# Differential attention, per-token attention and routed low-rank layers in one kernel: steps moved by one or two chunks in the per-token phase, one POOL step and a prefetch depth moved in the causal phase

## The chip, the cores and the metric

One core of a Trainium2 chip runs the whole program. The metric is the device time of one execution in microseconds (us), from several executions of the same program. The chip's engines are named as the profile names them: PE (TensorE, matmuls, with PEld for its weight loads), DVE (VectorE), ACT (ScalarE), POOL (GpSimd) and SP (which only issues DMAs here). Each engine works through its own list of instructions in order, and semaphores tie the lists together.

## The reference, cut to what matters

The input has 2 batches of 1024 tokens with 128 numbers each. Four layers follow one another, each added to its input after a layernorm:

```python
x = x + attn_a(layernorm(x))   # 16 heads, each with two causal softmax maps over 1024 tokens,
                               # out = softmax1 @ v - lambda * softmax2 @ v, rms norm, projection
x = x + ffn(layernorm(x))      # base matmul plus one of four low-rank experts per token
x = x + attn_b(layernorm(x))   # per token, below
x = x + ffn(layernorm(x))

# attn_b: H = 16 heads, C = 64 channels; everything is inside one token
Q = (x @ Wq + bq).reshape(b, s, H, C) * inv_sqrt_c
K = (x @ Wk + bk).reshape(b, s, H, C)
V = (x @ Wv + bv).reshape(b, s, H, C)
scores = einsum('bshq,bshk->bshqk', Q, K)       # a 64 x 64 outer product per token and head
scores = where(triu(ones((C, C)), 1), -inf, scores)
w = softmax(scores, axis=-1)
attn = einsum('bshqk,bshk->bshq', w, V)
return attn.reshape(b, s, HID) @ Wo + bo
```

In `attn_b` the score of query channel i and key channel j is the product q[i]*k[j], so the largest score of a row is the larger of q[i]*max(k[0..i]) and q[i]*min(k[0..i]). The kernel gets these maxima from a running maximum and a running minimum of the keys.

## The kernel before, in words

The program runs phases one after the other: a1 (load, layernorm, q/k/v), a2 (causal attention), a3 (rms norm and projection), f1, b (per-token attention), f2. The change touches a2 and b.

**Phase b** works on 16 tiles of 128 tokens. The scores of a tile are cut into 24 chunks, `c` = 0 to 23, of 256 to 2048 numbers per partition (token); chunks 0 to 15 are half 0 of the queries, 16 to 23 are half 1. The sizes in order are 2048, 256, 2048, 512, 2048, 768, 2048, 1024, 2048, 1280, 2048, 1536, 2048, 1792, 2048, 2048, and then 2048, 256, 1792, 512, 1536, 768, 1280, 1024. Every chunk passes through all four engines:

- DVE multiplies queries by keys into `p_ring` (L969, "product"), four chunks ahead (`AHEAD = 4`) of its own second step;
- POOL subtracts the row maxima `m` in place (L1059, "shift");
- ACT takes the exponential in place (L1097);
- PE adds up the exponentials by identity matmuls into a PSUM bank (L1160, the denominators), DVE multiplies them by the values into `ev_ring` (L1017), and PE adds those up in another bank (L1160, the numerators).

Written out by hand around the chunks are the steps that happen once or twice in a tile. Numbers such as `FINISH1_AT` name the chunk after which an engine does them; `it` is the tile in work:

- keys of tile it+1 on PE (`KEY_AT`), copied out of PSUM by ACT (`KEY_TAKEN_AT`); the same keys head by head on PE (`HJ_AT`, "hj"), scanned by DVE into running maxima and minima (`SCAN_AT`, L976 and L978), reordered by ACT with two copies (`TURN_BACK_AT`, L1083, "turned back"), and multiplied by the queries on DVE (`maxima`, L990, L991, L993; half 0 of the next tile after chunk 20, half 1 of this tile after chunk 12);
- the queries of half 1 on PE after chunk 11 (`Q1_AT`), those of half 0 of the next tile after chunk 19;
- the reciprocals of the denominators on ACT as exp(-ln(x)), with a table load ahead of either function (`invert`, L1075 and L1077): half 0 after chunk 20 of the tile, half 1 after chunk 4 of the next one;
- `finish` on DVE (L999), which multiplies the summed numerators by these reciprocals: half 0 after chunk 19, half 1 after chunk 3 of the next tile; then the output projection on PE (`PROJECT_AT`, L1169) and the residual addition on DVE (`RESIDUAL_AT`, L1004).

A linear step on PE is a matmul (L1125, which the profile shows as two records) and a small one for the bias (L1126). The first `maxima` product goes to `m`, the second to a PSUM bank `t`; before, `t` is bank `T_BANK`, which keys, hj and the projection use as well, and which is why `maxima` of half 1 waited for the keys to be taken, and hj for `maxima`.

**Phase a2** works on 16 jobs (a batch and a group of four score maps). In a job PE goes through 12 blocks of keys (`at` = 0 to 11, four score matmuls each, L492, 48 steps), ACT takes exponentials (L547), POOL zeroes the future part of the eight blocks on the diagonal (`mask`, L384, at 0, 1, 2, 3, 8, 9, 10, 11) and PE multiplies by the values (L505). Between the score matmuls PE works off a list of 26 items: 24 "max" items (scores for the row maxima, L449 and L453, each reduced by DVE, L564, from 256 to 1024 numbers wide), one "rows" item (L462, which puts the maxima of the next job into rows, after POOL has split them into three bf16 parts: `split`, L374 and L377) and one "turn" item. Two pairs of PSUM banks take the items in turn, so that an item on PE needs the one two places ahead of it to be reduced on DVE. `EARLY` is how many max items of job n+2 are worked off in job n; `EARLY_ROWS` is behind how many of these the rows item stands. After items 8 to 11 of a job DVE also does a `pad` (L573).

Of the kernel before, what the change touches and what calls it, by code (L numbers as in the profile page):

```python
# [44 lines left out]
H = 16  # L45
# [12 lines left out]
class Count:  # L58
# [8 lines left out]
    def at(self, it, k):  # L67

        return it * self.per + (self.first + k)
# [232 lines left out]
def phase_a2(nc, rows_q, rows_k, rq, rk_of_group, rk, v1, att, k, queries_spread, keys_spread):  # L302
# [4 lines left out]
    JOBS = BATCH * GROUPS  # L307
    with ExitStack() as ctx:
# [9 lines left out]
        ps = ctx.enter_context(nc.psum_tensor("a2_ps", [P, 8, 512], F32))  # L318
# [2 lines left out]
        U, G = len(units), len(groups)  # L321
        STEPS = 4 * G
        ST_SLOTS, ST_BANK, O_BANK, ITEM_BANK = 3, 0, 3, 4
        EARLY, EARLY_ROWS, TURN_ITEM, PAD_ITEM = 5, 3, 6, 8
        DIAGONAL = [at for at, (half, sbk) in enumerate(groups) if sbk * P >= 512 * half]
        masked = sem("masked", len(DIAGONAL))
        ready = sem("ready")
# [37 lines left out]
        @block.gpsimd  # L365
        def _(pool):
            def split(n):

                pool.wait_ge(item_taken.sem, number[("max", n, U - 1)] + 1)
                if n >= 1:  # L370
                    pool.wait_ge(item_psum.sem, number[("rows", n - 1, 0)] + 1)
                for part in range(3):
                    rows = mrows[:, :, M_ROW + 4 * part:M_ROW + 4 * part + 4]
                    nc.gpsimd.tensor_copy(rows, negm[:, n % 2]).then_inc(split_step.sem, 1)  # L374
                    pool.wait_ge(split_step.sem, split_step.at(n, 2 * part + 1))
                    if part < 2:
                        nc.gpsimd.tensor_tensor(negm[:, n % 2], negm[:, n % 2], rows, ALU.subtract).then_inc(split_step.sem, 1)  # L377
                        pool.wait_ge(split_step.sem, split_step.at(n, 2 * part + 2))

            def mask(n, at):  # L380

                pool.wait_ge(exp_done.sem, exp_done.at(n, 4 * at + 4))
                block_diagonal = ex[:, (G * n + at) % 3, :, 0:P]
                nc.gpsimd.affine_select(block_diagonal, block_diagonal, [[0, 4], [1, P]], ALU.is_ge, 0.0, base=0,  # L384
                                        channel_multiplier=-1).then_inc(masked.sem, 1)

            def combine(n):

                g, b = n // BATCH, n % BATCH
                pool.wait_ge(divided.sem, divided.at(n, 2))  # L390
                nc.gpsimd.tensor_scalar(oh[:, :, 1, :], oh[:, :, 1, :], k["lam"][:], None, ALU.mult).then_inc(out_step.sem, 1)
                pool.wait_ge(out_step.sem, out_step.at(n, 1))
                dst = att[:, b * NT:(b + 1) * NT, g * 2 * A_V:(g + 1) * 2 * A_V].rearrange("p n (v c) -> p n v c", v=2)
                heads = oh[:].rearrange("p (n v) s c -> p n v s c", n=NT)
                nc.gpsimd.tensor_tensor(dst, heads[:, :, :, 0, :], heads[:, :, :, 1, :], ALU.subtract).then_inc(out_step.sem, 1)

            nc.gpsimd.memset(mrows[:], 0.0).then_inc(ready.sem, 1)
            nc.gpsimd.tensor_scalar(k["wqkv"][:, 0, :], k["wqkv"][:, 0, :], 0.125, None, ALU.mult).then_inc(scaled.sem, 1)
            nc.gpsimd.tensor_scalar(k["bias"][0:HID // 32, :], k["bias"][0:HID // 32, :], 0.125, None, ALU.mult).then_inc(scaled.sem, 1)
            pool.wait_ge(scaled.sem, 2)  # L400
            for part in range(3):
                nc.gpsimd.tensor_copy(bias_parts[:, part, :], k["bias"][:]).then_inc(bias_step.sem, 1)
                pool.wait_ge(bias_step.sem, bias_step.next(0))
                if part < 2:
                    nc.gpsimd.tensor_tensor(k["bias"][:], k["bias"][:], bias_parts[:, part, :],
                                            ALU.subtract).then_inc(bias_step.sem, 1)
                    pool.wait_ge(bias_step.sem, bias_step.next(0))
            pool.wait_ge(ready.sem, 1)
            split(0)
            for n in range(JOBS):  # L410
                for at in DIAGONAL:
                    mask(n, at)
                    if at == 2 and n >= 1:
                        combine(n - 1)
                    if at == 9 and n + 1 < JOBS:
                        split(n + 1)
            combine(JOBS - 1)
            pool.wait_ge(out_step.sem, out_step.at(JOBS - 1, 2))

# [438 lines left out]
def phase_b(nc, x_all, k):  # L858
# [11 lines left out]
    BEGIN = (0, 16)  # L870
# [3 lines left out]
    Q_BANK, T_BANK, V_BANK, ACC_BANK = 0, 1, 2, 4  # L874
    HALF = HID // 2
    INVERT0_AT, INVERT1_AT = 20, 4
    FINISH0_AT, FINISH1_AT, PROJECT_AT, RESIDUAL_AT = 19, 3, 4, 6
    XT_AT, KEY_AT, KEY_TAKEN_AT = 5, (7, 9), (10, 12)
    HJ_AT, SCAN_AT, TURN_BACK_AT = (13, 15), (14, 16), 18
    Q1_AT, Q0_AT, V1_AT, V0_AT = 11, 19, 16, 23  # L880
    with ExitStack() as ctx:
        sb = lambda n, s, d=F32: ctx.enter_context(nc.sbuf_tensor("b_" + n, s, d))
# [19 lines left out]
        ps = ctx.enter_context(nc.psum_tensor("b_ps", [P, 8, 512], F32))  # L902
# [8 lines left out]
        key_taken = sem("key_taken", 2)  # L911
# [3 lines left out]
        m_step = sem("m_step", 6)  # L915
# [22 lines left out]
        def chunk(ring, c):  # L938

            half, j0, n = CH[c]  # L940
            return ring[:, c % ring.shape[1], 0:ROWS * n * H].rearrange("p (j i h) -> p j i h", j=ROWS, h=H)
# [9 lines left out]
        def over_queries(t, c):  # L951

            return t.unsqueeze(2).broadcast_to([P, ROWS, CH[c][2], H])
# [7 lines left out]
        def _(dve):  # L961
# [16 lines left out]
                nc.vector.tensor_tensor_scan(kmin[:, cols], k["reset_min"][:, 0:HALF], ps[:, T_BANK], 0.0,  # L978
                                             ALU.max, ALU.min).then_inc(scan_done.sem, 1)

            def maxima(it, half, last=False):

                q = ps[:, Q_BANK].rearrange("p (i h) -> p i h", h=H)
                t = ps[:, T_BANK].rearrange("p (i h) -> p i h", h=H)
                at = lambda r: r[:, half * FIRST:(half + 1) * FIRST, :]
                dve.wait_ge(q_psum.sem, q_psum.at(it, half + 1))
                dve.wait_ge(turned_back.sem, turned_back.at(it, 2))
                if half == 1 and not last:
                    dve.wait_ge(key_taken.sem, key_taken.at(it + 1, 2))
                nc.vector.tensor_tensor(m[:, half], q, at(kmaxr), ALU.mult).then_inc(m_step.sem, 1)  # L990
                nc.vector.tensor_tensor(t, q, at(kminr), ALU.mult).then_inc(m_step.sem, 1)  # L991
                dve.wait_ge(m_step.sem, m_step.at(it, 3 * half + 2))
                nc.vector.tensor_tensor(m[:, half], t, m[:, half], ALU.max).then_inc(m_step.sem, 1)  # L993
# [12 lines left out]
            def tile(it, buf, first, last):  # L1006
                for c in range(N):
                    coming = (it, buf, c + AHEAD) if c + AHEAD < N else None if last else (it + 1, 1 - buf, c + AHEAD - N)
                    begins = coming and coming[2] in BEGIN
                    if coming and not begins:  # L1010
                        multiply(*coming, first and c + AHEAD < N)
                    if c == 0:
                        dve.wait_ge(v_psum.sem, v_psum.at(it, 2))
                    dve.wait_ge(exp_done.sem, exp_done.at(it, c + 1))
                    if c >= EV_SLOTS or not first:
                        dve.wait_ge(ev_summed.sem, ev_summed.at(it, c - EV_SLOTS + 1))
                    nc.vector.tensor_tensor(chunk(ev_ring, c), chunk(p_ring, c), over_queries(values(c), c),  # L1017
                                            ALU.mult).then_inc(ev_done.sem, 1)
                    if begins:
                        maxima(coming[0], BEGIN.index(coming[2]), last)  # L1020
                        multiply(*coming, first and c + AHEAD < N)
                    if not first and c == FINISH1_AT:
                        finish(it - 1, 1)
                    if not first and c == RESIDUAL_AT:
                        residual(it - 1)
                    if c == FINISH0_AT:
                        finish(it, 0)
                    if not last and c in SCAN_AT:
                        scans(it + 1, SCAN_AT.index(c))
# [91 lines left out]
        def _(pe):  # L1121
# [51 lines left out]
            def tile(it, buf, first, last):  # L1173
                for c in range(N):
                    half = CH[c][0]
# [11 lines left out]
                        queries(it, buf, 1)  # L1187
                    if not last and c in HJ_AT:
                        if c == HJ_AT[0]:
                            pe.wait_ge(m_step.sem, m_step.at(it, 6))  # L1190
                        keys_by_head(it + 1, 1 - buf, HJ_AT.index(c))
                    if not last and c == V1_AT:
                        pe.wait_ge(ev_done.sem, ev_done.at(it, 16))
# [9 lines left out]
            for s in range(TILES // FT):  # L1203
                pe.wait_ge(xn_ready.sem, s + 1)
                for n in range(FT):
                    last = nc.tensor.transpose(ps[:, ACC_BANK + s, n * P:(n + 1) * P], xn[:, s * FT + n, :], k["ident"][:])
# [8 lines left out]
            vals(0, 0, 1)  # L1215
            vals(0, 0, 0)
            all_tiles(pe, tile)
            project(TILES - 1)

# [107 lines left out]
```

## Time and profile before

| | |
|---|---|
| device time, median of 3 | 2248.83 us (2248.59 to 2249.04) |
| the profiled execution: its own time | 2247.19 us |
| its span, first to last instruction | 2245.5 us |
| mean granted TensorE clock, share of full speed | 0.937 |
| busy in the span | PE 1893.1, DVE 1888.0, POOL 1415.5, ACT 1106.6 us |
| first and last POOL shift of phase b | 711.8 and 2172.3 us |
| first and last mask of phase a2 | 90.6 and 587.8 us |

Read a busy time of a whole program as a mean over phases: a2 and b are bounded by different engines. Where the profile says what ended an idle time, the engine named is the one whose result came last.

### The profile page before, as it was taken

To read this page: it belongs to the slowest core of one execution; us is meant where nothing else is said; L and a number is where in the kernel's file an instruction comes from. 1 tells how busy PE (TensorE), PEld (TensorE's weight loads), DVE (VectorE), ACT (ScalarE), POOL (GpSimd) and SP (SyncE) were. 2 spreads that over 40 slices of the span, in tenths; PEclk is the share of its full clock that TensorE was granted. 3 is DMA by queue.
4 is the path that set the end of the run, shared out by engine and by line. 5 is a ranking of instruction groups with operands and counts; after the bars stand their busy time and mean duration, and the time that the engine had idled before them with its cause. 6 is when DMAs were issued, how large, how long until landed. Compare 5 with 4: busy or idle time off the path is not lost. (4 is left out here: it accounts for less than half of the span.)

```text
span 2245.5 us, 35597 instructions
## 1 busy us (share of the span) xinstructions
PE 1893.1 (84%) x14176; PEld 1405.2 (63%) x14226; DVE 1888.0 (84%) x1607; ACT 1106.6 (49%) x1448; POOL 1415.5 (63%) x661
## 2 busy tenths in 40 slices
PE   2899999999565978889889898888888989889886
PEld 1344444443253767767778787776777777777785
DVE  6877888777345989989899899998999989999884
ACT  2366666666412454454545544445544555444540
POOL 5122222222113987978879788797897987979871
PEclk8899999999866999999999999999999989999996
DMA  3300000000000000000000000000000000000000
GB/s 96 61 7 6 8 8 8 5 5 1 1 0 0 1 1 1 1 2 1 1 2 1 1 1 2 1 1 2 1 1 2 1 1 1 2 1 1 1 1 19
DMA packets 10981, 14.46 MB, mean 6 GB/s; under 512 B 4656, under 2 KB 7632, under 8 KB 10672
## 3 DMA queue, kind: packets, MB, share of 16 engines
q1 hardware_dynamic: 9264, 11.31, 2.1%
q8 instruction: 126, 2.06, 0.4%
q10 hardware_dynamic: 1536, 0.63, 0.1%
q14 instruction: 55, 0.45, 0.1%
HBM read 4.57 MB, written 1.05 MB: 3 GB/s over the span
## 5 line engine op out<-in xcount | busy, mean ns | idle before, releaser
L1059 POOL TENSOR_TENSOR b_p_ring<-b_p_ring,b_m 128x2048 f32<-128x2048 f32 (+7 forms) x384 | 1251.4, 3300 | 244.3 <-DVE b_p_ring L969 243.0
L1097 ACT ACTIVATE b_p_ring<-b_p_ring 128x2048 f32<-128x2048 f32 (+7 forms) x384 | 532.3, 1411 | 654.1 <-POOL b_p_ring L1059 652.5
L1160 PE MATMUL b_ps<-k_ident,b_ev_ring 128*128 128x128 f32 (+6 forms) x4608 | 606.5, 283 | 162.9 <-DVE b_ev_ring L1017 157.5
L1160 PEld LDWEIGHTS b_ps<-k_ident,b_ev_ring 128*128 128x128 f32 (+6 forms) x4608 | 510.0, 139 | 237.2 <-DVE b_ev_ring L1017 211.2
L1017 DVE TENSOR_TENSOR b_ev_ring<-b_p_ring,b_ps 128x2048 f32<-128x2048 f32 (+7 forms) x384 | 634.1, 1655 | 5.7 <-PE b_ps L1126 4.0
L969 DVE TENSOR_TENSOR b_p_ring<-b_ps,b_key 128x2048 f32<-128x2048 f32 (+7 forms) x384 | 634.4, 1660 | 0.0
L1160 PE MATMUL b_ps<-k_ident,b_p_ring 128*128 128x128 f32 (+6 forms) x4608 | 588.0, 279 | 18.3 <-ACT b_p_ring L1097 12.6
L1160 PEld LDWEIGHTS b_ps<-k_ident,b_p_ring 128*128 128x128 f32 (+6 forms) x4608 | 521.9, 138 | 28.5 <-ACT b_p_ring L1097 12.9
L547 ACT ACTIVATE a_ex<-a_ps 128x512 f32<-128x512 f32 (+3 forms) x768 | 333.0, 497 | 200.5 <-PE a_ps L492 191.0
L564 DVE TENSOR_REDUCE a_negm<-a_ps 128x1 f32<-128x768 f32 (+7 forms) x384 | 353.3, 953 | 75.6 <-PE a_ps L453 72.7
L384 POOL TENSOR_SCALAR_AFFINE_SELECT a_ex<-a_ex 128x512 f32<-128x512 f32 x128 | 81.6, 638 | 372.6 <-ACT a_ex L547 371.1
L449 PE MATMUL a_ps<-rk,rq 128*128 128x512 bf16 (+3 forms) x751 | 190.8, 335 | 31.3 <-DVE rk L573 16.6
L492 PE MATMUL a_ps<-rq,rk 128*128 128x512 bf16 (+3 forms) x735 | 202.9, 329 | 6.9 <-ACT a_ex L547 5.5
L505 PE MATMUL a_ps<-a_ex,v 128*32 128x512 f32 (+3 forms) x1536 | 163.9, 499 | 1.1 <-POOL a_ex L384 1.1
L492 PEld LDWEIGHTS a_ps<-rq,rk 128*128 128x128 bf16 x768 | 64.0, 98 | 149.0 <-ACT a_ex L547 116.6
L1125 PE MATMUL b_ps<-k_wqkv,b_xt 128*128 128x512 f32 x256 | 138.1, 622 | 5.2 <-DVE b_kmin L978 2.4
L449 PEld LDWEIGHTS a_ps<-rk,rq 128*128 128x128 bf16 x768 | 66.5, 99 | 82.5 <-DVE a_negm L564 33.4
L999 DVE TENSOR_TENSOR b_oT<-b_ps,b_rden 128x512 f32<-128x512 f32 x32 | 22.1, 692 | 107.9 <-ACT b_rden L1077 107.9
L453 PE MATMUL a_ps<-k_mask,k_ident_b 128*128 128x128 bf16 x512 | 93.5, 224 | 0.0
L1083 ACT COPY b_kmaxr<-b_kmax 128x1024 f32<-128x1024 f32 x16 | 32.1, 2007 | 102.0 <-DVE b_kmin L978 102.0
L453 PEld LDWEIGHTS a_ps<-k_mask,k_ident_b 128*128 128x128 bf16 x512 | 50.3, 101 | 45.8 <-issue 5.0
L1126 PEld LDWEIGHTS b_ps<-bias,ones 3*128 3x128 bf16 x128 | 11.6, 91 | 101.9 <-issue 101.9
(163 smaller groups left out, 1076.8 us busy)
## 6 DMA issues: line engine op xcount, KB each, us to landing
rk_of_group<-rows_k SPq DMA_DIRECT2D x96, 32.0 KB, 2.0
rq<-rows_q SPq DMA_DIRECT2D x42, 64.0 KB, 2.4
k_wqkv<-in_wqkv SPq DMA_DIRECT2D x1, 2048.0 KB, 8.5
out<-x_all SPq DMA_DIRECT2D x4, 256.0 KB, 2.4
k_wo<-in_wo SPq DMA_DIRECT2D x1, 512.0 KB, 9.3
rq<-rows_q SPq DMA_DIRECT2D x12, 32.0 KB, 1.9
k_w_attn<-in_w_attn ACTq DMA_DIRECT2D x1, 192.0 KB, 2.8
k_reset_max<-in_reset_max ACTq DMA_DIRECT2D x1, 128.0 KB, 4.8
```

The lines of the kernel that those rows point to most:

```text
L449: nc.tensor.matmul(dst[:, 512 * at + c:512 * at + c + w], rq[:, g, b, t * P:(t + 1) * P], rk[:, n % 3, hh, c:c + w], start=True, stop=c + ...
L453: last = nc.tensor.matmul(dst[:, c:c + P], k["ident_b"][:], k["mask"][:], start=False, stop=True)
L492: nc.tensor.matmul(dst[:, 0:hi - lo], rk[:, n % 3, hh, sbk * P:(sbk + 1) * P], rq[:, g, b, lo:hi], start=True, stop=True).then_inc(st_psum ...
L505: last = nc.tensor.matmul(ps[32 * hh:32 * hh + 32, O_BANK, lo - 512 * half:512], v1[:, b * NT + sbk, 2 * g + hh // 2, :], ex[:, (G * n + a ...
L547: nc.scalar.activation(ex[:, (G * n + at) % 3, hh, 0:hi - lo], ps[:, ST_BANK + s % ST_SLOTS, 0:hi - lo], ACT.Exp).then_inc(exp_done.sem, 1)
L564: nc.vector.tensor_reduce(negm[:, n % 2, t, heads[0]:heads[-1] + 1], src, X, ALU.max, negate=True).then_inc(item_taken.sem, 1)
L969: nc.vector.tensor_tensor(chunk(p_ring, c), over_rows(ps[:, Q_BANK], c), over_queries(key[:, buf, j0:j0 + ROWS, :], c), ALU.mult).then_inc ...
L1017: nc.vector.tensor_tensor(chunk(ev_ring, c), chunk(p_ring, c), over_queries(values(c), c), ALU.mult).then_inc(ev_done.sem, 1)
L1059: nc.gpsimd.tensor_tensor(pc, pc, over_rows(m[:, half].rearrange("p i h -> p (i h)"), c), ALU.subtract).then_inc(shifted.sem, 1)
L1097: nc.scalar.activation(pc, pc, ACT.Exp).then_inc(exp_done.sem, 1)
L1125: nc.tensor.matmul(ps[:, bank], xt[:, buf], k["wqkv"][:, i, cols], start=True, stop=False)
L1160: last = nc.tensor.matmul(ps[0:width, bank, b // IB * P:(b // IB + 1) * P], rows[:, r, b:hi].rearrange("p i h -> p (i h)"), k["ident"][:], ...
```

## The change

In phase a2, five max items early become seven, the rows item moves two places back among them (so that it keeps its place in the list), and POOL's `split` for the next job stands ahead of the mask at 9 instead of behind it. In phase b, `finish` of half 1 moves from chunk 3 to 5, the projection from 4 to 6, the residual from 6 to 8, the keys from (7, 9) to (9, 11), their copies from (10, 12) to (12, 14), hj from (13, 15) to (14, 16), the scans from (14, 16) to (15, 17), and the turned copies from 18 to 20, where they stand behind `invert` of half 0. The scratch of `maxima` moves from `T_BANK` to the bank that sums the denominators of the same half; `maxima` of half 1 no longer waits for the keys of the next tile to be taken, and hj waits for that copy instead of for `maxima`. No instruction is added or taken away.

```diff
-        EARLY, EARLY_ROWS, TURN_ITEM, PAD_ITEM = 5, 3, 6, 8
+        EARLY, EARLY_ROWS, TURN_ITEM, PAD_ITEM = 7, 5, 6, 8
...
                 for at in DIAGONAL:
+                    if at == 9 and n + 1 < JOBS:
+                        split(n + 1)
                     mask(n, at)
                     if at == 2 and n >= 1:
                         combine(n - 1)
-                    if at == 9 and n + 1 < JOBS:
-                        split(n + 1)
...
-    FINISH0_AT, FINISH1_AT, PROJECT_AT, RESIDUAL_AT = 19, 3, 4, 6
-    XT_AT, KEY_AT, KEY_TAKEN_AT = 5, (7, 9), (10, 12)
-    HJ_AT, SCAN_AT, TURN_BACK_AT = (13, 15), (14, 16), 18
+    FINISH0_AT, FINISH1_AT, PROJECT_AT, RESIDUAL_AT = 19, 5, 6, 8
+    XT_AT, KEY_AT, KEY_TAKEN_AT = 5, (9, 11), (12, 14)
+    HJ_AT, SCAN_AT, TURN_BACK_AT = (14, 16), (15, 17), 20
...
-            def maxima(it, half, last=False):
+            def maxima(it, half):
...
-                t = ps[:, T_BANK].rearrange("p (i h) -> p i h", h=H)
+                t = ps[:, ACC_BANK + 2 * half + 1].rearrange("p (i h) -> p i h", h=H)
...
-                if half == 1 and not last:
-                    dve.wait_ge(key_taken.sem, key_taken.at(it + 1, 2))
...
-                            pe.wait_ge(m_step.sem, m_step.at(it, 6))
+                            pe.wait_ge(key_taken.sem, key_taken.at(it + 1, 2))
```

What stands where on ACT, from chunk 18 to chunk 21 of a tile of phase b. Before:

```order
L1097 ACTIVATE b_p_ring<-b_p_ring 128x1792
L1083 COPY b_kmaxr<-b_kmax 128x1024
L1083 COPY b_kminr<-b_kmin 128x1024
L1097 ACTIVATE b_p_ring<-b_p_ring 128x512
L1097 ACTIVATE b_p_ring<-b_p_ring 128x1536
L1075 ACT_TABLE_LOAD
L1075 ACTIVATE b_rden<-b_ps 128x512
L1077 ACT_TABLE_LOAD
L1077 ACTIVATE b_rden<-b_rden 128x512
L1097 ACTIVATE b_p_ring<-b_p_ring 128x768
```

Of the changed kernel, whose lines stand two lower here (L1095 is L1097 of before, L1081 is L1083, L1073 and L1075 are L1075 and L1077):

```order
L1095 ACTIVATE b_p_ring<-b_p_ring 128x1792
L1095 ACTIVATE b_p_ring<-b_p_ring 128x512
L1095 ACTIVATE b_p_ring<-b_p_ring 128x1536
L1073 ACT_TABLE_LOAD
L1073 ACTIVATE b_rden<-b_ps 128x512
L1075 ACT_TABLE_LOAD
L1075 ACTIVATE b_rden<-b_rden 128x512
L1081 COPY b_kmaxr<-b_kmax 128x1024
L1081 COPY b_kminr<-b_kmin 128x1024
L1095 ACTIVATE b_p_ring<-b_p_ring 128x768
```

The two turned copies moved from ahead of the exponentials of chunks 19 and 20 and of the reciprocals to behind them.

DVE in a tile inside the loop, from its second step of chunk 3 on (the 512-wide L1017). Before:

```order
L1017 TENSOR_TENSOR b_ev_ring<-b_p_ring,b_ps 128x512
L997 ISA
L998 ISA
L999 TENSOR_TENSOR b_oT<-b_ps,b_rden 128x512
L969 TENSOR_TENSOR b_p_ring<-b_ps,b_key 128x2048
```

Of the changed kernel, where L1015 is L1017 of before and L997 is L999:

```order
L1015 TENSOR_TENSOR b_ev_ring<-b_p_ring,b_ps 128x512
L969 TENSOR_TENSOR b_p_ring<-b_ps,b_key 128x2048
L1012 REGISTER_ALU
L1015 TENSOR_TENSOR b_ev_ring<-b_p_ring,b_ps 128x2048
L969 TENSOR_TENSOR b_p_ring<-b_ps,b_key 128x1280
L1012 REGISTER_ALU
L1015 TENSOR_TENSOR b_ev_ring<-b_p_ring,b_ps 128x768
L995 ISA
L996 ISA
L997 TENSOR_TENSOR b_oT<-b_ps,b_rden 128x512
```

`finish` of half 1 moved behind the products of chunks 8 and 9 and the second steps of chunks 4 and 5.

POOL in phase a2, in a job in the middle (three masks, at 3, 8 and 9, then the split of the next job). Before:

```order
L395 TENSOR_TENSOR att<-a_oh 128x8x16
L384 AFFINE_SELECT a_ex<-a_ex 128x4x128 x3
L374 CAST a_mrows<-a_negm 128x8x4
L377 TENSOR_TENSOR a_negm<-a_negm,a_mrows 128x32
L374 CAST a_mrows<-a_negm 128x8x4
L377 TENSOR_TENSOR a_negm<-a_negm,a_mrows 128x32
L374 CAST a_mrows<-a_negm 128x8x4
L384 AFFINE_SELECT a_ex<-a_ex 128x4x128 x5
```

Of the changed kernel:

```order
L395 TENSOR_TENSOR att<-a_oh 128x8x16
L384 AFFINE_SELECT a_ex<-a_ex 128x4x128 x2
L374 CAST a_mrows<-a_negm 128x8x4
L377 TENSOR_TENSOR a_negm<-a_negm,a_mrows 128x32
L374 CAST a_mrows<-a_negm 128x8x4
L377 TENSOR_TENSOR a_negm<-a_negm,a_mrows 128x32
L374 CAST a_mrows<-a_negm 128x8x4
L384 AFFINE_SELECT a_ex<-a_ex 128x4x128 x6
```

The five small instructions of the split moved ahead of one mask.

## Rows read from the trace of the kernel before

**Rows 1.** Windows, chunk 0 to chunk 0: PE, PEld, DVE, ACT, POOL busy, clock, DMA

```profile
983.66:1076.50 92.84, 80.45 (x616) 68.51 (x616) 85.53 (x62) 45.59 (x37) 78.23 (x24) 0.97 0.01 2
...
1168.89:1261.70 92.81, 83.96 (x616) 71.97 (x616) 85.52 (x62) 45.57 (x37) 78.18 (x24) 0.93 0.01 2
```

**Rows 2.** Waits in phase b (720 to 2190 us): total us, times, longest

```profile
DVE b_oT L999 <- ACT b_rden L1077: 107.9, 32, 6.0
ACT b_kmaxr L1083 <- DVE b_kmin L978: 91.9, 15, 6.4
...
DVE b_ev_ring L1017 <- PE b_ps L1126: 4.0, 8, 1.4
```

**Rows 3.** Timeline of DVE: start us, us, instruction [idle before it <-releaser]

```profile
961.02 1.75 DVE L969 TENSOR_TENSOR b_p_ring<-b_ps,b_key 128x1536 f32<-128x1536 f32 x1
...
977.01 0.69 DVE L999 TENSOR_TENSOR b_oT<-b_ps,b_rden 128x512 f32<-128x512 f32 x1 [3.57 <-ACT b_rden L1077]
...
979.28 0.68 DVE L990 TENSOR_TENSOR b_m<-b_ps,b_kmaxr 128x512 f32<-128x512 f32 x1
...
1005.51 0.69 DVE L999 TENSOR_TENSOR b_oT<-b_ps,b_rden 128x512 f32<-128x512 f32 x1 [3.54 <-ACT b_rden L1077]
...
1038.34 0.68 DVE L990 TENSOR_TENSOR b_m<-b_ps,b_kmaxr 128x512 f32<-128x512 f32 x1
```

**Rows 4.** Timeline of DVE at the end of phase b

```profile
2184.86 0.69 DVE L999 TENSOR_TENSOR b_oT<-b_ps,b_rden 128x512 f32<-128x512 f32 x1 [6.04 <-ACT b_rden L1077]
```

**Rows 5.** Timeline of ACT, same columns

```profile
967.24 2.01 ACT L1083 COPY b_kmaxr<-b_kmax 128x1024 f32<-128x1024 f32 x1 [6.39 <-DVE b_kmin L978]
969.16 2.05 ACT L1083 COPY b_kminr<-b_kmin 128x1024 f32<-128x1024 f32 x1
...
973.14 1.28 ACT L1075 ACT_TABLE_LOAD   x1
...
976.34 0.63 ACT L1077 ACTIVATE b_rden<-b_rden 128x512 f32<-128x512 f32 x1
...
1023.92 1.49 ACT L1097 ACTIVATE b_p_ring<-b_p_ring 128x1536 f32<-128x1536 f32 x1 [1.06 <-POOL b_p_ring L1059]
...
1030.27 0.57 ACT L1090 COPY b_key<-b_ps 128x512 f32<-128x512 f32 x1
```

**Rows 6.** Timeline of POOL: stretches that begin at chunks 20, 8 and 16

```profile
962.85 3.46 POOL L1059 TENSOR_TENSOR b_p_ring<-b_p_ring,b_m 128x1536 f32<-128x1536 f32 x1 [2.48 <-DVE b_p_ring L969]
...
1008.48 33.01 POOL L1059 TENSOR_TENSOR b_p_ring<-b_p_ring,b_m 128x2048 f32<-128x2048 f32 x8 [0.64 <-DVE b_p_ring L969]
1042.72 10.51 POOL L1059 TENSOR_TENSOR b_p_ring<-b_p_ring,b_m 128x2048 f32<-128x2048 f32 x4 [1.23 <-DVE b_p_ring L969]
```

**Rows 7.** Timeline of POOL: single shifts, of chunk 6 and of chunk 12

```profile
1000.95 4.55 POOL L1059 TENSOR_TENSOR b_p_ring<-b_p_ring,b_m 128x2048 f32<-128x2048 f32 x1
...
1023.83 4.59 POOL L1059 TENSOR_TENSOR b_p_ring<-b_p_ring,b_m 128x2048 f32<-128x2048 f32 x1
```

**Rows 8.** Timeline of PE: the queries of half 1 after chunk 11

```profile
1035.53 1.02 PE L1125 MATMUL b_ps<-k_wqkv,b_xt 128*128 128x512 f32 x2
1036.49 0.38 PE L1126 MATMUL b_ps<-bias,ones 3*128 3x512 bf16 x1
```

**Rows 9.** Waits of the whole span: PE for POOL's split

```profile
PE a_ps L462 <- POOL a_mrows L374: 19.4, 15, 2.3
```

**Rows 10.** Timeline of PE: one rows item of phase a2

```profile
337.16 0.61 PE L462 MATMUL a_ps<-k_ident_b,a_mrows 128*128 128x128 bf16 x8 [1.22 <-POOL a_mrows L374]
```

**Rows 11.** Timeline of POOL: the mask at 9 and the split's last instruction

```profile
335.00 0.64 POOL L384 TENSOR_SCALAR_AFFINE_SELECT a_ex<-a_ex 128x512 f32<-128x512 f32 x1 [1.83 <-ACT a_ex L547]
...
336.81 0.21 POOL L374 CAST a_mrows<-a_negm 128x32 bf16<-128x32 f32 x1
```

**Rows 12.** Groups of reduces, 90 to 590 us: busy, mean ns | idle before

```profile
L564 DVE TENSOR_REDUCE a_negm<-a_ps 128x2 f32<-128x1024 f32 x30 | 35.4, 1216 | 1.3 <-PE a_ps L453 1.3
...
L564 DVE TENSOR_REDUCE a_negm<-a_ps 128x2 f32<-128x512 f32 x28 | 19.4, 692 | 20.2 <-PE a_ps L453 20.2
```

More of the change, by code:

```diff
@@ L1019, in tile @@
                     if begins:
-                        maxima(coming[0], BEGIN.index(coming[2]), last)
+                        maxima(coming[0], BEGIN.index(coming[2]))
                         multiply(*coming, first and c + AHEAD < N)
```

## The prediction

> **What bounds the kernel now.** I began with windows that each run from POOL's first shift of a tile to that of the next. A tile of phase b takes 92.8 us, and in it DVE is busy 85.5 us, POOL 78.2, PE 80.5 to 84.0 and ACT 45.6 [rows 1]. So DVE is nearest to being full, with about 7.3 us idle. Sixteen such tiles are some 1480 of the 2245.5 us. The list of waits in phase b says where DVE's idle time is: 107.9 us in 32 waits of L999 (`finish`) for the reciprocal on ACT, and 4.0 us in 8 waits for the values from PE [rows 2]. The reader is to see that almost nothing else holds DVE up. It never waits there for POOL's shift or for a ring slot in any amount.
>
> The timeline then shows both places. At 977.01 `finish` of half 0 starts after 3.57 us of idle, at 1005.51 that of half 1 after 3.54 [rows 3]. For half 1 the order alone is to blame: `finish` stands behind chunk 3, the reciprocal behind ACT's chunk 4. For half 0 it is ACT's list. At chunk 18 ACT stands 6.39 us until DVE's second scan is done, then turns for 967.24 to 971.21, and only then come the exponentials of 19 and 20 and the reciprocal, which ends at 976.97 [rows 5].
>
> Phase a2 is bounded by PE. The one long PE wait there is 1.2 us a job for POOL's split, 19.4 us in 15 waits [rows 9, 10].
>
> **The change, part by part.**
>
> *Half 1 of `finish`, from 3 to 5.* The reciprocal stays behind chunk 4 on ACT, and DVE's second step of chunk 5 already needs ACT's chunk 5, which stands behind it. So `finish` finds the reciprocal done and its stall goes. What was queued behind it (products of chunks 8 and 9, on which POOL waited 0.64 us at chunk 8 [rows 6]) comes 3.54 us sooner. Projection, residual and keys move by the same two chunks and keep their spacing.
>
> *Half 0, by turning after the reciprocal.* I walk the tile around 960 us. DVE's product of chunk 20 ends at 961.02 + 1.75 = 962.77 [rows 3], and POOL's shift runs from 962.85 to 966.31 [rows 6]. The exponential of a 1536-wide chunk takes 1.49 [rows 5], so 967.8. Table loads, logarithm and exponential take 973.14 to 976.97, that is 3.83 [rows 5], so 971.6. DVE comes to `finish` at 977.01 - 3.57 = 973.4 [rows 3], 1.8 us later. The stall goes.
>
> The two copies follow. The scans, done at 967.2 now, come one chunk later, behind a 256-wide second step and one product, so about 1 us later; they no longer stop ACT. The copies take 3.97 (967.24 to 971.21) [rows 5], so they end at 975.6. DVE reaches `maxima` at 979.28 - 3.57 = 975.7 [rows 3]. The margin is 0.1 us, so this is what is late next. It rests on POOL reaching chunk 20 before its product. POOL waits there 2.48 us now. With DVE 3.54 sooner, POOL's waits of 0.64 and 1.23 at chunks 8 and 16 [rows 6] go, which moves POOL 1.87 ahead, so 2.48 - (3.54 - 1.87) = 0.8 us of that wait is left. That holds, closely.
>
> *The sum of both.* All waits of L999 but the last, which stands behind the last tile where nothing covers it (6.04 us [rows 4]): 107.9 - 6.0 = 101.9 us [rows 2]. This is 6.8 us a tile, so a tile should take 85.9 us, just above DVE's 85.5.
>
> *Keys and queries.* The second keys step now stands at chunk 11, ahead of the queries of half 1, which DVE wants in `maxima` at 1038.34 [rows 3]. They end at 1036.87 now, 1.47 ahead. A linear step takes 1036.87 - 1035.53 = 1.34 [rows 8], so the margin falls to 0.13. The lower bound of what this costs is nothing. The upper bound is one such step in every tile, 1.34 x 15 = 20 us, as when PE runs at 1.2 instead of 2.4 GHz there. I price the two thin margins (this, and the turned copies) by the nearest row of a step with no margin: DVE waits for the values in 8 of 16 tiles for 0.5 us each [rows 2], 0.25 a tile. Two of them in 15 tiles: 7.5 us.
>
> *Scratch in the denominators' bank, `maxima` without its wait.* L990 had no idle of note in the middle of the phase, so the removed wait gives nothing by itself; it lets the keys move. DVE reads and writes as much PSUM as before. Zero. In the new bank `finish` of the same half is already past when `maxima` comes, and PE's next sums there wait for the shift, so no one queues.
>
> *Split ahead of the mask at 9.* Mask 8 ends at 335.00 - 1.83 = 333.2. The split takes 335.64 to 337.02, or 1.4 [rows 11], so it could end at 334.6, provided the last max item is reduced, which now comes two items sooner. PE wants it at 337.16 - 1.22 = 335.9 [rows 10], and the mask at 9 still finds POOL free at 335.0. The 19.4 us go.
>
> *Seven early items.* They have a price. Behind the rows item and DVE's addition now stand items 768 and 1024 wide in place of 512 and 768, so DVE has 1216 - 692 = 0.52 us more to do there [rows 12], and PE may run only two items ahead. The pads likewise fall beside wider reduces. Bounds: nothing, and three such places (rows, start of the next job, pads), 1.57 a job, which is more than the 1.2 won. I take two, 1.05 x 15 = 16, so phase a2 gives 19.4 - 16 = 4 us (19 to -5).
>
> *Sum against the profiled execution:* 2245.5 - 101.9 + 7.5 - 4 = 2147 us of span. 1.7 us lie around the span (2247.19), and the median shown is 1.6 above that execution, so 2150.6. I forecast **2150 us**.
>
> **Two rules weighed.** A 2048-wide shift took 4.55 us while DVE stood idle for 3.54 us of it, and 4.59 under a busy DVE [rows 3, 7]: a full DVE costs POOL at most 0.9%, 0.7 us of 78.2, just inside the 0.8 us above. The Trainium skill (GPSIMD Engine Reference, Specifications) says that GpSimd shares its SBUF interfaces with VectorE and that they contend when VectorE works in a two-port mode or with two SBUF inputs. Both large DVE steps here have one input in PSUM, so by it nothing is lost; rule and row leave the sum as it is.
>
> The granted clock is 0.97 and 0.93 in two tiles with PE busy 80.5 and 84.0 us [rows 1]: part of each tile runs at 1.2 GHz. The Trainium skill (TensorE: Matmul & The Clock Gate, Part 1) holds that a busy TensorE is released from the slower clock. By that, with DVE's stalls gone, PE has fewer gaps, the thin margins would not be used up, and the 7.5 us fall away: 2143.
>
> **The rivals.**
>
> 1. *Turned copies late.* For it: 0.1 us of margin at the end of a chain over three engines. Against: ACT and POOL have no other work there. If POOL loses its 0.8 us and as much again, DVE waits about 1 us in 15 tiles: 2165; half of the copies' time (2.0) would give 2180.
>
> 2. *PE becomes the bound.* For it: 84.0 us of work in a tile at clock 0.93 against a new tile of 85.9, and 0.13 us ahead of `maxima`. Against: at full clock its work is under 80. At a mean clock of 0.95, 5% of 92.8 us run at half speed and 2.3 us of work are lost a tile. All on DVE's path: 2150 - 7.5 + 2.3 x 15 = 2177. Half of it: 2160.
>
> 3. *The half-0 stall stays.* If the reciprocal were late because of the denominators rather than ACT's list, 15 stalls of 3.57 us stay: 2150 + 54 = 2204. ACT shows no wait between the exponentials and L1075 in these rows, so this is unlikely. If both halves stayed, the change would do nothing: about 2245.
>
> 4. *Slower.* PE's second keys step at chunk 11 waits for the first copy of the keys, now behind ACT's chunk 12. PE comes there at 1035.53 - 3.54 = 1032.0, and the copy behind chunk 12 ended at 1030.84 [rows 5]: a margin of 1.15 us. Beyond it PE stands, the queries come late, and DVE stands at `maxima` one for one, with POOL and ACT behind it. It eats the whole gain (98 us, 6.5 a tile) once ACT's chunk 12 is 1.15 + 6.5 = 7.7 us later relative to DVE; at 9 us the time is 2150 + 15 x 7.85 = 2268. POOL would have to be as far behind, and it has 7.3 us to spare a tile.
>
> **How the numbers follow.** Forecast 0.64 (its own range 2128 to 2160: no cost at the margins and the full 19 in a2 give 2248.8 - 101.9 - 19.4 = 2127.5; the upper end has a2 at -5), rival 1 0.14, rival 2 0.12, rival 3 0.06 (0.02 of it with no gain at all), rival 4 0.04. Leaving out rivals 3 and 4 and the last ends of the others gives 2130 to 2175. A difference of 0.2% (4.5 us) is about what a measurement of this kernel can tell from none. Faster: 0.94. Within: 0.02. Slower: 0.04.
>
> **What would show it.** DVE's waits at `finish` should be one of 6 us at the end and little else. ACT's wait ahead of the turned copies should be gone. The tile should take 85.5 to 86.5 us with POOL at 78.2. `maxima` after chunks 12 and 20 shows rivals 2 and 1 as waits for PE and ACT. In phase a2 the 1.2 us ahead of L462 should be gone, and small waits of PE for L564 grown. I am wrong if DVE's stalls reappear at `maxima` with more than 1 us each, or if POOL's chunk 20 no longer waits for DVE.

## The result, and the profile after

The changed kernel takes 2136.05 us (median of 4, 2134.47 to 2138.50) against 2248.93 before: a ratio of 0.950, 95% interval 0.948 to 0.952. The forecast was 2150, range 2130 to 2175. The span of the profiled execution fell from 2245.5 to 2136.7 us, by 108.8.

Executions of one kernel differ by more than the four of this comparison show: beside the experiments below the kernel before took 2237.4 to 2249.0 us (one stray execution of 3711 us left out), the shortest at a mean granted clock of 0.948, the longest at 0.938. A difference of a few us between two kernels is therefore read from their traces here.

The windows of the changed kernel, one tile first and then fourteen tiles from chunk 0 to chunk 0 (busy us of PE, PEld, DVE, ACT, POOL, then the granted clock as a share of full speed, DMA share, GB/s):

```profile
961.58:1046.96 85.38, 77.45 (x616) 66.61 (x616) 85.31 (x62) 45.62 (x37) 78.23 (x25) 1.00 0.01 2
...
790.81:1986.09 1195.28, 1084.54 (x8624) 932.56 (x8624) 1194.33 (x855) 638.57 (x518) 1094.75 (x337) 1.00 0.01 1
```

The same fourteen tiles of the kernel before:

```profile
798.45:2094.83 1296.38, 1132.48 (x8624) 967.75 (x8624) 1196.88 (x855) 638.21 (x518) 1095.18 (x337) 0.96 0.01 1
```

A tile takes 85.38 us instead of 92.6, and DVE is busy 85.31 of them [rows 1 for before]. Its work is nearly the same (1194.3 against 1196.9 us in fourteen tiles); its idle time is gone. Fourteen tiles give 101.1 us of the 108.8. PE's clock, 0.96 before, is 1.00: it is at 2.4 GHz throughout these tiles. The first mask of phase a2 starts at 90.9 and the last at 582.0 us, 491.1 apart against 497.2, so a2 gives 6.1.

What DVE still waits for at `finish` (now L997), from the group of that line, and at the first product of `maxima` (now L988), total us and times:

```profile
  ACT b_rden L1075: 8.1, 2
```

```profile
  ACT b_kminr L1081: 4.6, 2
  PE b_ps L1124: 0.9, 1
```

The 8.1 are the end of the phase alone, 2.04 us in the last tile and 6.04 behind it [rows 4]. Of the 4.6, 3.9 stand ahead of the first tile, as before; the other 0.7 and the 0.9 for PE stand in the first tile, so in the fourteen tiles `maxima` never waits. The waits for the values from PE (4.0 us, [rows 2]) are not there at all.

The margins can be read tile by tile. DVE in the tile around 1120 us: the product of chunk 20, `finish` of half 0, `maxima` of the next tile:

```profile
1113.33 1.73 DVE L969 TENSOR_TENSOR b_p_ring<-b_ps,b_key 128x1536 f32<-128x1536 f32 x1
...
1125.64 0.68 DVE L997 TENSOR_TENSOR b_oT<-b_ps,b_rden 128x512 f32<-128x512 f32 x1
...
1127.96 0.69 DVE L988 TENSOR_TENSOR b_m<-b_ps,b_kmaxr 128x512 f32<-128x512 f32 x1
```

POOL and ACT in the same stretch:

```profile
1115.14 5.26 POOL L1057 TENSOR_TENSOR b_p_ring<-b_p_ring,b_m 128x1536 f32<-128x1536 f32 x2 [0.55 <-DVE b_p_ring L969]
```

```profile
1123.35 0.63 ACT L1075 ACTIVATE b_rden<-b_rden 128x512 f32<-128x512 f32 x1
...
1125.84 2.02 ACT L1081 COPY b_kminr<-b_kmin 128x1024 f32<-128x1024 f32 x1
```

The reciprocal is done at 1123.98, 1.66 us ahead of `finish`. The turned copies are done at 1127.86 and DVE starts `maxima` at 1127.96, without idle. POOL's wait for chunk 20 has shrunk from 2.48 to 0.55 us [rows 6]. On PE the keys step and the queries of half 1 stand one behind the other after chunk 11:

```profile
1094.96 1.02 PE L1123 MATMUL b_ps<-k_wqkv,b_xt 128*128 128x512 f32 x2
1095.91 0.39 PE L1124 MATMUL b_ps<-bias,ones 3*128 3x512 bf16 x1
1096.23 1.13 PE L1123 MATMUL b_ps<-k_wqkv,b_xt 128*128 128x512 f32 x2
1097.29 0.39 PE L1124 MATMUL b_ps<-bias,ones 3*128 3x512 bf16 x1
```

They end at 1097.68, and DVE's `maxima` of half 1 follows at 1097.77: 0.09 us ahead.

### The profile page after: what moved, and what is told of

Read it like the earlier page. It is cut to its first block and busy times, and to the rows that moved or that the text cites. A ratio compares the mean times of both kernels' runs of the same rounds, so it can differ in the third digit from the quotient of the medians.

```text
span 2136.7 us, 35583 instructions
## 1 busy us (share of the span) xinstructions
PE 1847.3 (86%) x14162; PEld 1368.3 (64%) x14226; DVE 1884.3 (88%) x1607; ACT 1108.5 (52%) x1448; POOL 1414.5 (66%) x661
## 5 line engine op out<-in xcount | busy, mean ns | idle before, releaser
L1095 ACT ACTIVATE b_p_ring<-b_p_ring 128x2048 f32<-128x2048 f32 (+7 forms) x384 | 532.7, 1412 | 640.8 <-POOL b_p_ring L1057 640.8
L1158 PE MATMUL b_ps<-k_ident,b_ev_ring 128*128 128x128 f32 (+6 forms) x4608 | 579.7, 276 | 121.7 <-DVE b_ev_ring L1015 121.5
L1015 DVE TENSOR_TENSOR b_ev_ring<-b_p_ring,b_ps 128x2048 f32<-128x2048 f32 (+7 forms) x384 | 634.1, 1655 | 1.7 <-ACT b_p_ring L1095 1.7
L1158 PEld LDWEIGHTS b_ps<-k_ident,b_ev_ring 128*128 128x128 f32 (+6 forms) x4608 | 491.3, 135 | 183.3 <-DVE b_ev_ring L1015 159.1
L1158 PE MATMUL b_ps<-k_ident,b_p_ring 128*128 128x128 f32 (+6 forms) x4608 | 567.9, 273 | 19.5 <-ACT b_p_ring L1095 12.5
L1158 PEld LDWEIGHTS b_ps<-k_ident,b_p_ring 128*128 128x128 f32 (+6 forms) x4608 | 504.7, 135 | 26.1 <-ACT b_p_ring L1095 12.8
L384 POOL TENSOR_SCALAR_AFFINE_SELECT a_ex<-a_ex 128x512 f32<-128x512 f32 x128 | 81.6, 638 | 364.4 <-ACT a_ex L547 363.9
L449 PE MATMUL a_ps<-rk,rq 128*128 128x512 bf16 (+3 forms) x738 | 186.5, 332 | 37.2 <-DVE rk L573 16.7
L505 PEld LDWEIGHTS a_ps<-a_ex,v 128*32 128x32 f32 x1536 | 30.4, 108 | 40.2 <-ACT a_ex L547 19.6
L976 DVE TENSOR_TENSOR_SCAN b_kmax<-k_reset_max,b_ps 128x512 f32<-128x512 bf16 x32 | 38.9, 1215 | 15.2 <-PE b_ps L1124 15.2
```

The lines of the kernel that those rows point to most:

```text
L449: nc.tensor.matmul(dst[:, 512 * at + c:512 * at + c + w], rq[:, g, b, t * P:(t + 1) * P], rk[:, n % 3, hh, c:c + w], start=True, stop=c + ...
L505: last = nc.tensor.matmul(ps[32 * hh:32 * hh + 32, O_BANK, lo - 512 * half:512], v1[:, b * NT + sbk, 2 * g + hh // 2, :], ex[:, (G * n + a ...
L1095: nc.scalar.activation(pc, pc, ACT.Exp).then_inc(exp_done.sem, 1)
L1158: last = nc.tensor.matmul(ps[0:width, bank, b // IB * P:(b // IB + 1) * P], rows[:, r, b:hi].rearrange("p i h -> p (i h)"), k["ident"][:], ...
```

## The experiments

The questions were which edit gives what, whether the moves that had no price in the sum are needed, and whether the two margins of a tenth of a microsecond are real. All times are medians beside runs of the kernel before on the same chip.

**Phase a2 in two parts.** Split alone, in the kernel before:

```diff
                 for at in DIAGONAL:
+                    if at == 9 and n + 1 < JOBS:
+                        split(n + 1)
                     mask(n, at)
...
-                    if at == 9 and n + 1 < JOBS:
-                        split(n + 1)
```

> The kernel before with POOL's split ahead of the mask at 9 and nothing else. Theory 1 (the split's place is what PE waited for, and the seven early items cost part of it back): the 1.22 us ahead of L462 go in 15 jobs, so phase a2 gets 15 to 19 us shorter and the job 30.4 us long against 31.67; the time is 2230 to 2234, which is a larger gain in phase a2 than the 5.7 us that the changed kernel shows there. Rival (the last max items come too late without the two extra early ones): the split still waits for them, L462 keeps most of its 1.2 us, and the time stays within 4 us of before.

Measured: 2229.68, ratio 0.993 (0.991 to 0.995). Early items alone:

```diff
-        EARLY, EARLY_ROWS, TURN_ITEM, PAD_ITEM = 5, 3, 6, 8
+        EARLY, EARLY_ROWS, TURN_ITEM, PAD_ITEM = 7, 5, 6, 8
```

> The kernel before with seven early items, the rows item behind the fifth, and the split left behind the mask at 9. Theory 1: the two extra items cost PE waits for DVE's reduces of 0.5 to 1 us a job and win nothing, because the split still waits for the mask at 9: slower by 7 to 16 us, 2256 to 2265. Rival: they are what brought the gain of phase a2 (split ready earlier), and the time falls by about 6 us to 2243.

Measured: 2254.1, ratio 1.0039 (1.0023 to 1.0055): slower, by little more than a measurement can tell, and by 2 us less than the least that was expected. The group of the mask (L384, first and last start us) for the two kernels, split alone first:

```profile
L384 POOL TENSOR_SCALAR_AFFINE_SELECT a_ex<-a_ex x128: 634/634/645, 88.1 to 568.3; 128x512 f32<-128x512 f32 x128
```

```profile
L384 POOL TENSOR_SCALAR_AFFINE_SELECT a_ex<-a_ex x128: 634/635/644, 90.9 to 594.1; 128x512 f32<-128x512 f32 x128
```

First to last mask is 480.2 us with the split alone (17.0 less than the 497.2 of before) and 503.2 with the early items alone (6.0 more). A job in the middle takes 30.29 and 32.21 us, against 31.67 before and 31.14 in the changed kernel. So the split is the gain. The seven early items cost 0.54 us a job by themselves, and with the split ahead of the mask they take 0.85 us a job back (31.14 - 30.29). PE's waits in a2 show where: with the early items alone its weight loads wait 33.6 us in 81 times for DVE's reduces, 20.8 in 53 before:

```profile
PEld a_ps L449 <- DVE a_negm L564: 33.6, 81, 0.8
...
PE a_ps L462 <- POOL a_mrows L374: 16.1, 15, 2.2
```

and the wait for the split stays (16.1 against 19.4 us, [rows 9]). The mask at 9 still stands ahead of the split, so earlier max items gain little there.

**Phase b in two parts.** The turned copies alone, then `finish` of half 1 alone, in the kernel before:

```diff
-    HJ_AT, SCAN_AT, TURN_BACK_AT = (13, 15), (14, 16), 18
+    HJ_AT, SCAN_AT, TURN_BACK_AT = (13, 15), (14, 16), 20
```

> The kernel before with the two turned copies on ACT behind chunk 20 instead of 18 and nothing else. Theory 1 (the two stalls at finish are independent): the 3.57 us stall of half 0 goes in 15 tiles, 53 us, half 1 keeps its 3.2 us; 2249 - 53 = 2196, a tile of 88.9 us, ACT's wait for the scans (92 us) gone. Rival (POOL bounds once one stall is gone, so that the second stall grows by what the first loses): the tile stays above 91 us, time above 2225. Second rival (turned copies late at maxima): the copies end after DVE comes to L990, which then waits 1 us or more a tile: 2210 or more.

```diff
-    FINISH0_AT, FINISH1_AT, PROJECT_AT, RESIDUAL_AT = 19, 3, 4, 6
+    FINISH0_AT, FINISH1_AT, PROJECT_AT, RESIDUAL_AT = 19, 4, 4, 6
```

> The kernel before with finish of half 1 behind chunk 4 instead of 3 and nothing else (projection, residual, keys, scratch bank as before). The reciprocal ends at 1005.0 in the tile shown, and DVE would be through chunk 4's second step at 1007.0 without its stall. Theory 1: one chunk is enough, the stall of half 1 goes in 15 tiles, 48 us, and half 0 keeps 3.6 us: about 2201, a tile of 89.2 us. Rival (the projection on PE, which stands behind chunk 4 and now waits for a later finish, pushes the residual and the keys back, so that the move needs the others): PE or DVE waits at the projection or residual grow by over 1 us a tile, time 2215 or more.

Measured: 2193.93 (ratio 0.977, 0.974 to 0.979) and 2198.47 (0.979, 0.977 to 0.982), 53 and 48 us below before, near the 2196 and 2201 that were expected. DVE's waits at L999 between 720 and 2060 us, turned copies alone and `finish` alone:

```profile
DVE b_oT L999 <- ACT b_rden L1077: 49.6, 14, 3.8
```

```profile
DVE b_oT L999 <- ACT b_rden L1077: 53.3, 15, 3.6
```

Each kernel keeps one half's stalls whole and has lost the other's. The tile is 89.0 and 89.2 us long. Neither stall was hiding the other, and POOL was no bound behind the first. Both together, two numbers:

> The kernel before with two numbers changed: finish of half 1 behind chunk 4, turned copies behind chunk 20. Theory 1 (these two moves are the whole gain of phase b; scratch bank, keys, hj and scans were not needed for it): both stalls go, tile 85.4 to 85.6 us, time 2144 to 2148, as much below before as the changed kernel is in phase b. Rival (the other moves make room for them: with PE's keys at 7 and 9, and its hj step at 13 waiting for maxima, PE or the T_BANK steps get too late at the faster pace): tile 86.5 or more, DVE waits at L990 or L976, time 2162 or more.

Measured: 2140.42 (ratio 0.953, 0.951 to 0.956), below the 2144 to 2148 expected. Its fourteen tiles:

```profile
788.04:1983.66 1195.62, 1086.10 (x8624) 934.60 (x8624) 1194.48 (x855) 638.92 (x518) 1094.50 (x336) 1.00 0.01 1
```

That is 85.40 us a tile, with the keys at 7 and 9 and the scratch in `T_BANK`. In phase b the scratch bank and the moves of projection, residual, keys, hj and scans give nothing that two numbers don't.

**The changed kernel with five early items:**

> The changed kernel with five early items and the rows item behind the third, as before. Theory 1 (the seven early items cost PE waits for DVE, 0.86 us a job by the two single changes): phase a2 gets 11 to 13 us shorter, job 30.3 us, time 2123 to 2126. Rival (the two changes of phase a2 only work together in the changed kernel): 2136 or more.

Measured: 2124.06 (ratio 0.946, 0.943 to 0.948), 12 us below the changed kernel, job 30.29 us. In the traces phase a2, first to last mask, falls from 491.1 to 479.6 us, and PE's weight loads wait 21.0 us in 53 times for DVE's reduces, where the changed kernel has 33.5 in 80.

**The margins.** The turned copies one chunk later still (`TURN_BACK_AT` 21) in the changed kernel:

> The changed kernel with the turned copies one chunk later, behind ACT's chunk 21. Theory 1 (the copies end with a margin of about 0.1 us ahead of maxima): the exponential of a 768-wide chunk, 0.75 us, now stands ahead of them, and DVE waits 0.6 to 0.75 us at L988 in 15 tiles; tile 86.0 to 86.1, time 2145 to 2147. Rival (the margin is larger than read, since DVE's order or ACT's overlap hide more): no wait, 2136 to 2138.

Measured: 2150.54 (ratio 0.957, 0.955 to 0.960), its waits of DVE in phase b:

```profile
DVE b_m L988 <- ACT b_kminr L1081: 11.1, 15, 1.4
DVE b_ev_ring L1015 <- PE b_ps L1124: 1.0, 4, 0.4
DVE b_m L988 <- PE b_ps L1124: 0.8, 1, 0.8
```

The wait is 1.41 us in the first tile (0.66 in the changed kernel) and 0.68 to 0.71 in each of the others, for an instruction of 0.75 us: all that was left to absorb it is the margin of a tenth. The time is 3.5 us above the upper end of what was expected. PE's clock has slower stretches again (8 in the fourteen tiles, mean 0.99; none in the changed kernel), and there are waits for PE, 1.8 us, of which the changed kernel has only one of 0.9. That DVE's stalls bring the slower stretches isn't shown: the next run has a longer stall in every tile and none of them.

The queries' linear step done twice after chunk 11, in the changed kernel and in the one with two numbers:

```diff
+                if half == 1:
+                    linear(Q_BANK, buf, 0, half)
                 linear(Q_BANK, buf, 0, half).then_inc(q_psum.sem, 1)
```

> The changed kernel with the linear step of the queries of half 1 done twice on PE after chunk 11 (the second overwrites the first with the same numbers), 1.3 us more of PE. Theory 1 (behind the keys step, the queries end 0.1 us ahead of maxima): DVE waits 1.0 to 1.3 us at L988 after chunk 12 in every tile; tile 86.4 to 86.7, time 2152 to 2158. Rival (PE catches up elsewhere and the margin is larger than read): under 0.3 us a tile, time 2136 to 2141.

> The kernel with two numbers changed (finish 4, turned copies 20, keys still at 7 and 9), and the same doubled step. Theory 1 (here the queries have about 1.4 us to spare, since no keys step stands in the same chunk): no or under 0.3 us of wait a tile, tile 85.4 to 85.7, time 2138 to 2146, the same as with two numbers alone. Rival (PE's total work, now 1.3 us more a tile, decides and not the place): as much slower as the changed kernel gets, 15 us or more.

Measured: 2153.75 (ratio 0.959, 0.957 to 0.962) and 2144.59 (0.956, 0.953 to 0.958). The first one's wait, then the second one's:

```profile
DVE b_m L988 <- PE b_ps L1124: 19.5, 15, 2.2
```

```profile
DVE b_m L990 <- PE b_ps L1126: 2.2, 3, 0.9
```

The same work on PE costs 1.3 us in every tile where the keys step stands ahead of the queries, and nothing in 12 of 15 tiles where it doesn't. In the first of the two kernels PE stays at 2.4 GHz in all fourteen tiles, though DVE waits 1.23 us in each. PE's total is not the bound; the place is.

**The scratch bank.** The changed kernel with `t` in `T_BANK` and the two old waits:

```diff
-                t = ps[:, ACC_BANK + 2 * half + 1].rearrange("p (i h) -> p i h", h=H)
+                t = ps[:, T_BANK].rearrange("p (i h) -> p i h", h=H)
...
+                if half == 1 and not last:
+                    dve.wait_ge(key_taken.sem, key_taken.at(it + 1, 2))
...
-                            pe.wait_ge(key_taken.sem, key_taken.at(it + 1, 2))
+                            pe.wait_ge(m_step.sem, m_step.at(it, 6))
```

> The changed kernel with maxima's scratch back in T_BANK, with the old waits: maxima of half 1 for the second copy of the keys of the next tile, hj for maxima. Theory 1 (the bank is free of charge by itself and only allows the keys to come later): with the copy now behind ACT's chunk 14 while maxima stands behind DVE's chunk 12, DVE waits 3.5 to 4.5 us a tile at L990; tile 89 to 90 us, time 2190 to 2205. Rival (ACT is far enough ahead of DVE that the copy is done): under 0.5 us a tile, 2136 to 2144.

Measured: 2222.54 (ratio 0.990, 0.987 to 0.992), more than was expected:

```profile
DVE b_m L990 <- ACT b_key L1090: 64.8, 15, 6.5
DVE b_kmax L976 <- PE b_ps L1126: 19.5, 25, 1.0
```

The first row is the expected wait, 4.3 us a tile. The second I had missed: hj on PE now waits for the late `maxima`, and DVE's scans for hj. 64.8 + 19.5 = 84.3 of the 86.5 us. So the bank gives nothing where the keys are early (the kernel with two numbers), and without it the later keys cost those 84 us.

**The version that the runs point to.** The kernel before with three edits (split ahead of the mask at 9, `finish` 4, turned copies 20), and the same with the last job's split left behind its mask:

> The kernel before with three edits: finish of half 1 behind chunk 4, turned copies behind chunk 20, the split ahead of the mask at 9. Theory 1 (the rest of the change does nothing, or costs): tile 85.4, job 30.3 us, time 2122 to 2127, about 12 us below the changed kernel, all from the job being 0.86 us shorter. Rival (the edits of the two phases or the missing moves interact): over 2132.

```diff
-                    if at == 9 and n + 1 < JOBS:
+                    if at == 9 and n + 2 < JOBS:
                         split(n + 1)
...
+                    if at == 9 and n + 2 == JOBS:
+                        split(n + 1)
```

> The same with the split of the last job left behind the mask at 9. In the changed kernel POOL stands 5.0 us in that split with the mask at 9 behind it, and PE 3.9 us for the mask. Theory 1: the wait of 3.9 us goes, and the last interval between first masks falls from 34.4 us by 2 to 3 us, 2120 to 2124 in all. Rival (PE would wait for the split itself as much): no change.

Measured: 2121.43 (ratio 0.945, 0.943 to 0.948) and 2122.36 (0.9445, 0.9425 to 0.9465). Both medians lie some 14 us below the changed kernel's, with far fewer edits. They were taken on another chip, and by the ratios it is some 10 us; the traces show 10.9 us in phase a2 (480.2 against 491.1) and nothing in phase b. The last interval between first masks falls from 34.6 to 31.6 us in the profile, as expected, but the medians of these two overlap, so that those 3 us are shown in the trace only. In the changed kernel this cost is one wait of POOL in the last job's split, and one of PE behind it:

```profile
550.16 0.21 POOL L374 CAST a_mrows<-a_negm 128x32 bf16<-128x32 f32 x1 [5.00 <-DVE a_negm L564]
```

```profile
552.46 0.84 PE L505 MATMUL a_ps<-a_ex,v 128*32 128x384 f32 x4 [3.94 <-POOL a_ex L384]
```

The fourteen tiles of the kernel with three edits hold one more fact:

```profile
781.24:1976.52 1195.28, 1096.85 (x8624) 954.92 (x8624) 1194.32 (x855) 638.71 (x518) 1094.36 (x337) 0.98 0.01 1
```

PE's mean clock is 0.98 here, below the changed kernel's 1.00, and the tile is 85.38 us all the same. What decides is where in the tile a stretch at 1.2 GHz lies. Here there are 14, one of them at the start of the first of these tiles and the others 24 us into a tile, and DVE waits for PE after none of them. One of them, and one that ends 7.0 us into a tile of the kernel before, with the DVE step behind it:

```profile
891.20:894.60 3.40, 3.40 (x18) 3.40 (x18) 3.40 (x3) 0.77 (x1) 3.40 (x1) 0.50 0.00 0
```

```profile
1165.70:1175.94 10.24, 8.49 (x41) 7.29 (x40) 10.21 (x10) 2.22 (x2) 7.05 (x3) 0.50 0.01 3
...
1178.82 2.29 DVE L1017 TENSOR_TENSOR b_ev_ring<-b_p_ring,b_ps 128x2048 f32<-128x2048 f32 x1 [1.38 <-PE b_ps L1126]
```

PE makes the values for half 0 some 9 us into the tile, behind the sums that the slow stretch delays, and DVE needs them next. In the kernel before it was only there that a slower PE reached DVE.

## Why the prediction was right, and where it was off

- **The bound, DVE's two stalls a tile, and that both go: right.** Of 32 waits of L999, 30 are gone; left are 2.0 us in the last tile (0.5 before) and the 6.0 behind it. Shown by the trace and by each half alone. The sum had 101.9 us; 107.9 - 8.1 = 99.8 it was.
- **The walk of half 0: right to a tenth.** Reciprocal 1.8 us ahead of `finish` forecast, 1.66 found. Copies 0.1 ahead, 0.1 found, and both the later copies and the doubled queries showed that nothing else stood behind these margins. POOL's wait at chunk 20: 0.8 forecast, 0.55 found.
- **The price of the two thin margins, 7.5 us: mis-sized.** It was taken from the 8 waits for the values, 0.5 us each, as if a thin margin would fail in half the tiles. Measured are 1.5 us at L988 in the whole phase (0.7 and 0.9). And the 8 waits themselves, which the sum left standing, went as well: 4.0 us. In the trace before, the step that waited began 2.8 to 4.2 us after the end of a stretch at 1.2 GHz in all 8, and the changed kernel has none of these stretches in its fourteen tiles. I had the row (clock 0.97 and 0.93) and took the waits as belonging to the place, not to the clock. Nor are they a loss beside `finish`. Two more traces have phase b as before, those with the split alone and with the early items alone. The waits for the values come to 3.3 and 2.3 us there, those of L999 to 108.4 and 109.7, and the fourteen tiles to 1296.3 and 1296.4, as before: what DVE lost to the values, `finish` waited less. So without the stalls of `finish` the sum had those 112 us to take off, and not 107.9.
- **The rule weighed.** The Trainium skill (TensorE: Matmul & The Clock Gate, Part 1) was weighed and gave 2143, 7 us nearer than the sum; the trace of the changed kernel agrees with it, with PE's busy share from 0.87 to 0.91 and the clock from 0.96 to 1.00. By the mean over the tiles it doesn't hold for the kernel with three edits (0.92, clock 0.98). How much of its nearness is luck stays open: apart from one in the changed kernel with five early items, after which DVE waited for nothing, no trace has a slow stretch beside both thin margins.
- **Phase a2, 4 us: right in sign, its two terms mis-sized.** Removed 19.4 forecast, 17.0 measured, since the last job's split now holds up its mask (PE 3.9 us), which I had not walked. The early items' cost 16 forecast; with the split ahead it is 17.0 - 6.1 = 10.9. The two errors cancel in part, so that 4 came near 6.1 by some luck.
- **The rest of the difference.** Span: 2147.1 forecast, 2136.7 measured, 10.4 less. (With 1.7 and 1.6 the sum is 2150.4; the 2150.6 is a slip.) The terms above are 6.0 + 4.0 - 2.1 + 2.1 = 10.0. All but one of them made the forecast too long. The other 4 us of the median lie in the choice of executions: the profiled one was 1.6 us under its median before, and 2.45 over it after.
- **The rivals.** Turned copies late and PE as the bound did not come, but both were near: 0.75 us more on ACT, or 1.3 on PE, each brought the time to 2151 to 2154. Rival 2's price was mis-worked: a mean clock of 0.95 means 10% of the time at half speed and not 5%, so 4.6 us of work lost a tile and 2150 - 7.5 + 4.6 x 15 = 2212, half of it 2177, in place of 2177 and 2160. The slower one (keys late at chunk 11) left a single wait of PE for a copy of the keys, 0.7 us in the first tile (0.4 before). The 0.2% that the prediction took as the least difference to be told looks too small: the kernel before alone spread over 11.6 us, 0.5%.
- **GpSimd beside a full DVE: right.** POOL is busy 78.23 us a tile in both kernels, with DVE at 85.31 of 85.38. The loss of up to 0.7 us did not come.

Not tried: why the last max items' order costs 0.85 us a job, item by item. That the cost is PE waiting for reduces is read from the waits; which of the places carries it stays open.

## What to carry to other kernels

When an engine is nearly full and its idle time hangs on one kind of instruction, ask for each such wait what stands ahead of the releasing step in its own engine's list. Here two numbers (one step one chunk later, the turned copies behind the reciprocal instead of ahead of it) gave the whole of phase b, and the remaining moves only used up margins. Walk a moved step at the last and the first pass of its loop too, where the work that covers it is missing. A price taken from waits in a trace should first be checked against the clock of those moments, and a wait that another wait behind it absorbs is no price of its own.

## What was not expected of the hardware

PE was at 2.4 GHz throughout fourteen tiles at a busy share of 0.91 (1084.5 of 1195.3 us), where it had 0.87 and a clock of 0.96 before. But the kernel with three edits, with a busy share of 0.92, had 0.98, and its phase b is line for line that of the kernel with two numbers, which had 1.00. In the fourteen tiles PE was at 1.2 GHz for 82 to 96 us in the four traces that keep the stall of half 0 ahead of `finish` (before, split alone, early items alone, `finish` alone), for 31 with the turned copies alone, and for 0 to 48 with neither stall and nothing else added. So most of it goes with the stall of half 0, but the order of the code alone does not set it; what else does stays open.

The stretch from the last mask of a2 to the first shift of b, which no edit touches, varied between 118.6 and 125.5 us over the profiles, and with it the clock: 0.67 in the two traces with 118.6 us, 0.59 in the one with 125.5. That this is a source of the spread between executions of one kernel is likely, but not shown, as only one execution of each was traced.
